# Attention in a fused mixer, linear, attention and SwiGLU block: probability blocks split on ScalarE and GpSimd and turned by a DMA, in place of TensorE transposes

## The reference

```python
q = einsum('bth,oh->bto', x, Wq)      # 32 query heads of 128
k = einsum('bth,oh->bto', x, Wk)      # 8 key heads, each for 4 query heads
v = einsum('bth,oh->bto', x, Wv)
q = q * cos + rotate_half(q) * sin
k = k * cos + rotate_half(k) * sin
scores = einsum('bkgtd,bksd->bkgts', qg, k) / sqrt(128)
attn = softmax(where(causal, scores, -inf), axis=-1)
out = einsum('bkgts,bksd->bkgtd', attn, v)
x = layernorm(x + einsum('bto,ho->bth', out, Wo))
```

## Time and profile before

| | us |
|---|---|
| median of 3 runs | 2485.62 |
| lowest and highest | 2484.69, 2487.72 |
| profiled execution, its own time | 2484.75 |
| its span | 2482.8 |
| TensorE busy | 2378.8 |
| VectorE busy | 1787.9 |
| ScalarE busy | 1591.7 |
| GpSimd busy | 1232.0 |
| first to last `ohi`, 64 items | 1635.9 to 2325.9 |

### The profile page before, as it was taken

How to read it: one execution, slowest core, us unless ns; L and a number is a source line. 1 busy time by engine, 2 the same in 40 slices (tenths; PEclk the granted TensorE clock), 3 DMA queues, 4 the chain that set the end, 5 groups by cost and what they waited for, 6 DMA issues and landing times. The chain is left out here.

```text
span 2482.8 us, 48888 instructions
## 1 busy us (share of the span) xinstructions
PE 2378.8 (96%) x15424; PEld 1368.9 (55%) x15624; DVE 1787.9 (72%) x3234; ACT 1591.7 (64%) x3327; POOL 1232.0 (50%) x986
## 2 busy tenths in 40 slices
PE   6999999999999999999999998879999999999797
PEld 3555555555555555555555555445555555555443
DVE  6777777777777777777777776577777777788522
ACT  7676776776776776776776775265665656656422
POOL 4455555555555556556556459344434343454223
PEclk8999999999999999999999999999999999999999
DMA  7343343343343343343343341230110110100000
GB/s 248 108 129 111 108 128 111 108 133 105 113 132 107 110 133 109 106 137 109 102 140 109 119 151 56 103 124 1 43 43 1 44 44 1 43 18 1 1 0 34
DMA packets 113827, 218.79 MB, mean 88 GB/s; under 512 B 9632, under 2 KB 43040, under 8 KB 111360
## 3 DMA queue, kind: packets, MB, share of 16 engines
q1 hardware_dynamic: 113536, 215.28, 26.6%
HBM read 212.10 MB, written 3.15 MB: 87 GB/s over the span
## 5 line engine op out<-in xcount | busy, mean ns | idle before, releaser
L256 DVE SCALAR_TENSOR_TENSOR xc<-bank,taps,xc 128x511 f32<-128x511 f32 (+2 forms) x384 | 284.7, 742 | 44.6 <-ACT xc L243 27.4
L984 ACT ACTIVATE E<-wq,cst 128x128 f32<-128x128 f32 x1024 | 311.8, 390 | 2.2 <-PEq L298 2.2
L1268 POOL TENSOR_TENSOR xw<-xt,wdec 128x384 f32<-128x384 f32 x128 | 106.4, 832 | 327.3 <-DVE xt L1119 163.7
L1277 POOL TENSOR_TENSOR acc<-acc,sq 128x512 f32<-128x512 f32 x112 | 172.0, 1536 | 186.8 <-ACT sq L996 186.8
L1911 POOL TENSOR_TENSOR qT<-qT,qrot 128x512 f32<-128x512 f32 x64 | 81.3, 1270 | 368.6 <-DVE qrot L1801 368.6
L1161 DVE SCALAR_TENSOR_TENSOR u<-xc,D,bank 128x512 f32<-128x512 f32 x128 | 95.6, 747 | 210.3 <-PE bank L813 198.8
L1100 DVE TENSOR_TENSOR E<-E,cbm 128x1024 f32<-128x1024 f32 x128 | 242.9, 1898 | 0.8
L61 PE MATMUL bank<-xhi,wx 128*128 128x512 f16 x640 | 242.5, 379 | 0.0
L60 PE MATMUL bank<-xlo,wx 128*128 128x512 f16 x640 | 242.5, 379 | 0.0
L59 PE MATMUL bank<-xhi,wx 128*128 128x512 f16 x640 | 242.5, 379 | 0.0
L1263 POOL TENSOR_TENSOR ecs<-ecs,xcC 128x768 f32<-128x768 f32 x128 | 234.1, 1829 | 0.4 <-POOLq L298 0.4
(11 more groups left out here) (237 smaller groups left out, 6299.4 us busy)
## 6 DMA issues: line engine op xcount, KB each, us to landing
wq<-cs_rows SPq DMA_DIRECT2D x128, 512.0 KB, 4.1
ecs<-ecs_rows SPq DMA_DIRECT2D x128, 384.0 KB, 3.6
wx<-in_w_xbc SPq DMA_DIRECT2D x80, 256.0 KB, 2.7
wz<-in_w_z SPq DMA_DIRECT2D x64, 256.0 KB, 2.7
wo<-in_w_o SPq DMA_DIRECT2D x64, 256.0 KB, 4.0
wq<-in_wq SPq DMA_DIRECT2D x8, 1024.0 KB, 5.7
awo<-in_wo SPq DMA_DIRECT2D x8, 1024.0 KB, 5.0
wkv<-in_wkv SPq DMA_DIRECT2D x8, 512.0 KB, 3.7
```

The source lines that it names most:

```text
L256: self.nc.vector.scalar_tensor_tensor(out=dst[:, d:T], in0=self.k.bank[bank][:, 0:T - d], scalar=self.taps[:, bass.ds(g, 1), b, j, 3 - d:4 ...
L984: ins = nc.scalar.activation(E[t.i % 4][:, h, c], sc.csr[t.i % 2][:, h, c * P:(c + 1) * P], ACT.Relu, scale=-1.0, bias=head(sc.cst, t, c, h))
L1277: nc.gpsimd.tensor_tensor(acc[t.b][:], acc[t.b][:], sq[:], ALU.add).then_inc(acc_done, 1)
```

## The change

The transposes of the probabilities leave TensorE. ScalarE normalises the four row blocks of `probs` and then copies each to its leading fp16 half in a new buffer `ph` (20 blocks of 128 columns, leading halves and rests interleaved). GpSimd subtracts and writes the rests. SyncE then issues one DMA transpose of the 128 x 2560 fp16 buffer to `pt`, and `attend` reads both halves from there. `ph` has two buffers, `pt` and `probs` one each. The casts from PSUM to `pthi` and the subtractions on VectorE go.

The freed banks 5 and 6 join the projection ring, which has four banks now. The order within bodies changes: on TensorE projections come first, the scores follow the query projection, the output quarter comes before `attend`; on ScalarE `exps(n + 2)` comes before `ohi(n)`, and waits until the rests of item `n + 1` are written, since `probs` has one buffer; the value's leading half is read from PSUM and its rest is made by VectorE, after `maxima`. `add_output` comes before `olo`. The SwiGLU weights are loaded in 15 pieces behind the transposes of the first 15 items, and the scale of the down projection is loaded in the SwiGLU part.

```diff
 @block.sync
+                def turn(n, h):
+                    sp.wait_ge(p_lo, n + 1)
+                    sp.sem_inc(step, 1)
+                    if not (isinstance(n, int) and n == 0):
+                        sp.wait_ge(pv_ready, n)
+                        sp.sem_inc(step, 1)
+                    sp.dma_start_transpose(out=pt[:], in_=ph[h % 2][:]).then_inc(pt_in, 16)
...
-                load_swiglu(k, io, sp)
+                turn(0, 0)
...
+                            if later(g, b, h, 1):
+                                turn(n + 1, h + 1)
+                            if isinstance(g, int) and g < 2:
+                                load_swiglu(k, io, sp, n)
 @block.tensor, attend and body
-                        pe.wait_ge(pt_lo, 3 * n + min(j, 2) + 1)
+                    pe.wait_ge(pt_in, 16 * n + 16)
...
-                            turn(n, h, [0], None)
-                            turn(n, h, [1], None)
...
+                                if kind == "q":
+                                    m = later(g, b, h, 2)
+                                    scores(item(*m), *m)
...
-                            turn(n, h, [2, 3], 3 * n + 1)
                             attend(n, g, b)
-                            for i, (kind, what) in enumerate(uses):
-                                if kind == "o":
...
 @block.scalar
+                    wait(act, p_lo, n)
                     for i in (3, 2, 0, 1):
...
+                def leading_p(n, h):
                     act.wait_ge(exp_done, n + 1)
                     act.wait_ge(rsum_done, n + 1)
+                    wait(act, pt_in, 16 * n - 16)
+                    for i in (3, 2, 1, 0):
+                        nc.scalar.activation(probs(i), probs(i), ACT.Copy, scale=rsum[h % 2][:, i:i + 1]).then_inc(p_norm, 1)
+                    for j, i in enumerate((3, 2, 1, 0)):
+                        act.wait_ge(p_norm, 4 * n + j + 1)
+                        nc.scalar.copy(leading_blocks(h, i), probs(i)).then_inc(p_hi, 1)
...
+                            if later(g, b, h, 1):
+                                leading_p(n + 1, h + 1)
                             if later(g, b, h, 3):
                                 leading_q(n + 3, h + 3)
+                            if later(g, b, h, 2):
+                                exps(n + 2, h + 2)
...
                             act.wait_ge(pv_ready, n + 1)
                             nc.scalar.activation(ohi[b][:, h], k.bank[7][:, :], ACT.Copy,
                                                  scale=1.0 / P_SCALE).then_inc(ohi_done, 1)
-                            if later(g, b, h, 2):
-                                exps(n + 2, h + 2)
 @block.vector
-                        nc.vector.tensor_copy(v[:], k.bank[bank][:, :].rearrange("p (t d) -> p t d", d=P)).then_inc(v_ok, 1)
+                        dve.wait_ge(kv_hi, 2 * u + 2)
+                        nc.vector.tensor_tensor(vlo[b][:], bank[:, :].rearrange("p (t d) -> p t d", d=P), vhi[b][:],
+                                                ALU.subtract).then_inc(v_lo, 1)
...
-                def rest_of_p(n, u):
-                    bank, at, size = EVAC[u]
-                    dve.wait_ge(pt_hi, 3 * n + u + 1)
-                    nc.vector.tensor_tensor(ptlo[:, at:at + size], k.bank[bank][:, 0:size], pthi[:, at:at + size],
-                                            ALU.subtract).then_inc(pt_lo, 1)
 @block.gpsimd
+                def rest_of_p(n, h):
+                    for j, i in enumerate((3, 2, 1, 0)):
+                        pool.wait_ge(p_hi, 4 * n + j + 1)
+                        out = ph[h % 2][:, 5 * i * P:(6 * i + 1) * P].rearrange("p (b t) -> p b t", t=P)
+                        ins = nc.gpsimd.tensor_tensor(out, probs(i), leading_blocks(h, i), ALU.subtract)
+                    ins.then_inc(p_lo, 1)
...
                             if later(g, b, h, 2):
                                 rest_of_q(n + 2, h + 2)
+                            if later(g, b, h, 1):
+                                rest_of_p(n + 1, h + 1)
                             if h == 2 and not is_last(g, b):
                                 rest_of_k(g * NB + b + 1, 1 - b)
-                                rest_of_v(g * NB + b + 1, 1 - b)
                             if later(g, b, h, 3):
                                 add_q(n + 3, h + 3)
```

More of the change, by code:

```diff
@@ L1513, in attention @@
         krot = sb("krot", [P, T])
[L1514 removed]
+        pr = sb("probs", [P, 1280])
         qhi, qlo = ([sb(f"q{n}{i}", [P, T], F16) for i in range(4)] for n in ("hi", "lo"))
@@ L1593, in _ @@
                 aw.load_wo(sp, 1, 1)
-                load_swiglu(k, io, sp)
+                turn(0, 0)
                 def body(g, s, p):
[L1598 to L1603, removed]
+                    for b in range(NB):
+                        for h in range(QH):
+                            n = item(g, b, h)
+                            if later(g, b, h, 1):
+                                turn(n + 1, h + 1)
+                            if isinstance(g, int) and g < 2:
+                                load_swiglu(k, io, sp, n)
+                            if b == 0 and h == QH - 1 and not (isinstance(g, int) and g in (0, NG - 1)):
+                                sp.wait_ge(proj_ready, ring(g, 0, QH - 1, 1)[0] + 1)
+                                aw.load_wo(sp, g + 1, 1 - s)
+                            if b == 1 and h == 0 and not (isinstance(g, int) and g >= NG - 2):
+                                sp.wait_ge(proj_ready, ring(g, 1, 0, 0)[0] + 1)
+                                aw.load(sp, g + 2, s)
                 pairs(sp, body)
@@ L1692, in body @@
+                                if kind == "q":
+                                    m = later(g, b, h, 2)
+                                    scores(item(*m), *m)
                             m = later(g, b, h, 2)
-                            if m:
+                            if m and not later(g, b, h, 3):
                                 scores(item(*m), *m)
                             attend(n, g, b)
-                            for i, (kind, what) in enumerate(uses):
-                                if kind == "o":
-                                    ahead, bank = ring(g, b, h, i)
-                                    pe.wait_ge(proj_free, ahead - 1)
-                                    if what == 0:
-                                        pe.wait_ge(w_ok, W_PIECES * (g + b))
-                                    output(1 - b, bank, s if b else 1 - s, what)
@@ L1871, in body @@
                                 scales(n + 1, h + 1)
-                            for u in range(2):
-                                rest_of_p(n, u)
                             for i, (kind, what) in enumerate(uses):
@@ L1887, in body @@
                                                            op1=ALU.subtract).then_inc(pv_free, 1)
-                            for i, (kind, what) in enumerate(uses):
-                                if kind == "o":
-                                    ahead, bank = ring(g, b, h, i)
-                                    add_output(1 - b, ahead, bank, what, g * NB + b - 1)
                             if is_last(g, b):
```

184 lines of the change are left out of this document (88 added, 96 removed).

## The result

The changed kernel took 2628.69 us (median of 4 runs, 2625.89 to 2632.46), the kernel before 2485.34 in the same comparison: a ratio of 1.0576, 95% interval 1.0558 to 1.0594. The forecast was +45 us, within 2478 to 2690; the measured difference is +143. The direction and the range hold, the size is off by a factor of three.

The account below looks back on a forecast made before the run. Attention, bound by TensorE before, would be bound by an 11.0 us chain an item through ScalarE, VectorE and GpSimd; 60 intervals, 15 units' extras and the ends sum to 732.7 against 690.0, with the start +45: 2530 us, range 2478 to 2690.

Parts of the forecast that it names:

- Key and value bodies: Extra time in bodies with `h == 1` (2 x 0.53 and about 1.0) and `h == 2` (1.11); a unit takes 47.2 us.
- the loop as summed: Attention's chain from `ohi` to `ohi` through VectorE, ScalarE and GpSimd: 11.0 us an item; chance 0.60.
- The plain loop: The same chain in a body without key and value: 11.0 us, against 9.66 before.
- The rival in which TensorE stays the bound: Attention's chain closes within 9.7 us, so the transposes are gained whole: 70 us less, 2415; chance 0.11.
- the one with the DMA as the loop: One `pt` buffer makes the transpose bind from 9.2 us on; at 12 us +180, 2665; chance 0.24.
- The price of step 3: GpSimd's rests of the probabilities, 1280 columns an item: 2.8 us taken, bounds 2.4 and 4.5.
- The chain's upper end: Attention's chain with GpSimd's rests at their upper price: 62 x 1.7 = +107, up to 2637 us.
- The key and value body: Body with `h == 1`: two more ScalarE casts, 2 x 0.53, and about 1.0 for VectorE, on top of 11.0 us.
- The clock: Rival: idling TensorE is granted the lower clock throughout attention, +380 or more, 2870; at 0.96 nothing; chance 0.05.
- The DMA: Transpose of the probabilities, 640 KB an item: 5.5 us taken, landing in 4 to 7, covered up to 9.2.
- The ends: First `ohi` 3 us later; at attention's end 9.9 us for item 61's body and 15.2 for the last two items.

Follow-up runs that it names:

- the kernel of 2498.3: Changed kernel with GpSimd's key rest and query sum put ahead of the probabilities' rests; 2498.30 us, ratio 1.0050.
- the filler: Changed kernel plus 24 overwritten matmuls on TensorE before each unit's first scores, while it waits for the key's rest; 2612.89 us, ratio 1.0508.
- the best kernel: Changed kernel with key rest and query sum first on GpSimd, output's cast ahead of exponentials on ScalarE, weight splits moved earlier; 2464.83 us, ratio 0.9911.

## Why the forecast had the sign and a third of the size

**The step that failed** stands in "Key and value bodies": "With `h == 2`, `rest_of_k` (1.11) stands between `rest_of_p` and `add_q`." It charges the displaced instruction by its length on GpSimd's own path to the query sum. What it left out is who waits for the key's rest itself: TensorE's scores of the next unit, in the same body, with mask, maxima and exponentials behind them. That chain closes in 17.0 us on average over the 15 bodies, not 12.11, and moving that one instruction brought 87 us back. With it moved the kernel stands at 2541.6, 12 us off the forecast of 2530. So the loop as summed is right and this term was mis-sized: 1.11 in place of some 6 us a unit (17.03 - 11.0), of which 5.4 went with the order. That the kernel with it moved comes within 12 us of the forecast is in part luck: its bodies with `h == 2` are 6.7 us below their sum and the others 20.1 above theirs.

**The plain loop** holds in every step: `ohi` to scalings 1.80, scalings 1.83, the rests start 0.68 after the first copy and take 3.00, the query sum 1.26, cast and exponentials in turn, 11.14 in all against 11.0. The rival in which TensorE stays the bound is out. So is the one with the DMA as the loop.

**The price of step 3** came out at 3.04 us for 1280 columns, near the 2.8 chosen and far from the upper bound of 4.5. The Trainium skill (GPSIMD Engine Reference, Specifications) names contention with VectorE instructions that have two SBUF inputs; the long ones beside these rests read one operand from PSUM, and by that rule the trace agrees with a price near the lower one. The chain's upper end was summed with a slip that changes nothing: 62 x 1.7 is 105, not 107.

**The key and value body** was 14.7 us short over 15 units. The sum there took TensorE's work as covered, while a weight split on GpSimd (1.90) stands ahead of the query's rest in every second unit, and TensorE waits 3.5 us for it on average (24.5 in 7). The eight of these bodies without the split take 12.9 us on average, near the forecast's 13.06, and the seven with it 15.3. Moving splits gained 8.5 us in the kernel of 2498.3.

**The clock** "costs nothing" at 0.96 in the prediction. It cost 16 us at least: not as a level of the whole stretch, but in the stretch of each unit that follows a long idle one. Where the filler held the clock at 1.00 the scores took half the time, and the wait stayed.

**The DMA** landed in 4.9 us, expected 5.5 in a span of 4 to 7, and is covered. **The ends** gave +4.3 behind item 60 and about 3 us ahead of the first `ohi`, which were not taken apart. What sets the floor of 14.3 us in the best kernel's body with key and value stays open, and so does what keeps its plain bodies at 9.8 us on average, where the prediction has 8.57 of work for TensorE; its key cast waits there for the key's sum on GpSimd (73.1 us in 15), and the one attempt on this kernel to move that cast away, made together with another order on VectorE, lost more than it gave.

## What to carry to other kernels

When each engine runs an order written by hand, follow every moved instruction to all of its readers, those of the next unit too, and close each loop that comes out; an instruction of 1.2 us behind four that take 3 cost 5.4 us a unit because a whole chain hung on it. A gain taken off a busy engine is only had if no loop through the others closes above the new bound: work out the loop per kind of body, not for the plain one with additions. And a transfer that is free in one order is waited for in another, so a reordering must be costed with the transfers.

## What the runs showed of the hardware

The transposing DMA of 128 x 2560 fp16, SBUF to SBUF, landed in 4.8 to 6.7 us. Queue 1 in the 6 us around one, and its issue (packets, MB, share of 16 engines):

```profile
q1 hardware_dynamic: 2592, 0.66, 58.0%
...
pturned<-phalves SPq DMA_TRANSPOSE x1, 4.8
```

Two windows of 1 us of the changed kernel, the first within a transpose, the second within plain loads of weights (last two columns, DMA share and GB/s; a share above 1 says that times of packets overlap):

```profile
2103.00:2104.00 1.00, 1.00 (x7) 0.49 (x5) 0.69 (x1) 1.00 (x3) 0.00 (x0) 1.00 1.17 219
2126.00:2127.00 1.00, 1.00 (x4) 0.42 (x3) 0.00 (x0) 1.00 (x4) 0.00 (x0) 0.50 0.98 406
```

The Trainium skill (Advanced Engine Details and Errata, X-Bar Transpose) gives 350 to 400 GB/s, as for plain transfers; the trace disagrees, since the plain loads reach that and a transpose mostly moves about half (a few short stretches show up to 291), and the measurement decides. Its issue held SyncE's queue for 3.06 us (2.93 to 3.70), which nobody waited for here. TensorE's clock fell within an idle stretch of 6 us from 1.00 to 0.50, and 24 matmuls without use were worth 16 us.
